# Plain loads and TensorE turns for the first three x, fewer identity products, and shift rows ahead of the second queries

## The reference

```python
qkv = x @ Wqkv + bqkv
q, k, v = jnp.split(qkv, [D, D + KV], axis=-1)          # 16 heads of q, 4 of k and v, tiled to 16
scores = jnp.einsum('bqhd,bkhd->bhqk', q, k) / HD
out = jnp.einsum('bhqk,bkhd->bqhd', softmax(scores), v).reshape(b, s, D) @ Wout + bout
x = layernorm(x + out)
gate, up = jnp.split(jnp.einsum('bsd,hd->bsh', x, ternary_quant(w_gate_up)), 2, axis=-1)
hn = rms_norm(jax.nn.silu(gate) * up)
x = layernorm(x + jnp.einsum('bsh,dh->bsd', hn, ternary_quant(w_proj)))
```

## Time and profile before

| | |
|---|---|
| time, median of 3 runs | 571.05 us (570.61 to 571.38) |
| time of the profiled execution | 570.28 us |
| its span, from the first to the last instruction | 568.3 us |
| mean granted TensorE clock | 0.984 |
| busy in the span | TensorE 92%, VectorE 78%, ScalarE 64%, GpSimd 59% |
| chain that ended last | TensorE 47%, GpSimd 19%, issue 15%, VectorE 10% |

### The profile page before, as it was taken

One profiled execution on the slowest core, in us unless ns is written; L12 is line 12 of the kernel. 1 busy time (PEld: TensorE's weight loads), 2 busy tenths in 40 slices (PEclk: granted clock), 3 DMA queues, 4 the chain that ended last, 5 costly groups with the idle time before them and its releaser, 6 DMA issues.

```text
span 568.3 us, 13548 instructions
## 1 busy us (share of the span) xinstructions
PE 524.5 (92%) x4148; PEld 444.7 (78%) x4148; DVE 442.4 (78%) x1002; ACT 366.0 (64%) x738; POOL 335.5 (59%) x517
## 2 busy tenths in 40 slices
PE   4687999899999999999999999999999999999883
PEld 4677778688888888888888888888888888777772
...
GB/s 227 140 142 123 56 125 76 104 71 110 52 116 60 125 30 145 54 126 73 105 96 100 96 89 107 74 115 63 119 37 155 10 152 48 21 40 1 19 20 37
DMA packets 83379, 49.16 MB, mean 86 GB/s; under 512 B 39680, under 2 KB 83328, under 8 KB 83328
## 3 DMA queue, kind: packets, MB, share of 16 engines
...
## 4 chain that ended last, share of the span: by engine, by line
PE 47%; POOL 19%; issue 15%; DVE 10%; ACT 3%; DMA 3%; SPq 1%; ACTq 1%; POOLq 0%; DVEq 0%
PE ffn_ps L588 12%; PE short_ps L514 8%; PE pv_ps L616 7%; PE short_ps L560 6%; PE exp_ps L569 5%; PE down_ps L601 5%; POOL sq_sum L1015 5%; POOL h_lo L1010 4%; POOL rstd L999 2%; DVE row_max L834 2%; DVE h_f L910 2%; DVE gated L903 2%; POOL attB L403 1%; POOL k_p L1034 1%; DMA q_st<-shift_lo 1%
## 5 line engine op out<-in xcount | busy, mean ns | idle before, releaser
L834 DVE TENSOR_REDUCE row_max<-short_ps 128x2 f32<-128x512 f32 x256 | 174.0, 682 | 60.6 <-PE short_ps L560 60.0
L1010 POOL TENSOR_TENSOR h_lo<-h_f,h_hi 128x256 fp32r<-128x256 f32 x128 | 94.5, 739 | 179.7 <-ACT h_hi L737 179.5
L761 ACT ACTIVATE probs<-exp_ps 128x1024 f32<-128x1024 f32 x128 | 130.7, 1021 | 44.5 <-PE exp_ps L569 43.9
L560 PE MATMUL short_ps<-k_st,q_st 65*128 65x256 f32 x512 | 108.5, 296 | 3.6 <-DVE row_max L834 3.3
L746 ACT ACTIVATE tanh<-ffn_ps 128x256 f32<-128x256 f32 x120 | 45.7, 381 | 96.9 <-PE ffn_ps L588 96.9
L560 PEld LDWEIGHTS short_ps<-k_st,q_st 65*128 65x128 f32 x512 | 88.5, 193 | 15.1 <-issue 2.4
L588 PE MATMUL ffn_ps<-x1T_hi,wguT 128*128 128x256 f32 x480 | 80.8, 291 | 9.9 <-DVE h_f L910 9.3
L569 PE MATMUL exp_ps<-q_st,k_st 67*128 67x512 f32 x256 | 81.6, 400 | 3.3 <-DMA q_st<-shift_lo 3.2
L601 PE MATMUL down_ps<-wpT,h_hi 128*128 128x256 f32 x256 | 79.2, 332 | 3.7 <-POOL h_lo L1010 3.5
L588 PE MATMUL ffn_ps<-x1T_lo,wguT 128*128 128x256 f32 x480 | 78.0, 285 | 0.2 <-DVE x1T_lo L823 0.2
L588 PEld LDWEIGHTS ffn_ps<-x1T_hi,wguT 128*128 128x128 f32 x480 | 65.1, 189 | 16.0 <-issue 10.9
(11 more groups left out here) (104 smaller groups left out, 831.2 us busy)
## 6 DMA issues: line engine op xcount, KB each, us to landing
q_st<-q_dram SPq DMA_DIRECT2D x128, 128.0 KB, 4.1
...
res<-in_L_attn_x_dram SPq DMA_DIRECT2D x16, 256.0 KB, 2.9
out_dram<-y_out SPq DMA_DIRECT2D x16, 256.0 KB, 2.9
...
wgu_raw<-in_L_ffn_w_gate_up_dram SPq DMA_DIRECT2D x8, 256.0 KB, 6.4
...
```

The costliest lines, as they stand in the source:

```text
L560: last = pe.matmul(bank[:, t * S:(t + 1) * S], q_st[0:PAD, st.par, head, t * P:(t + 1) * P], k_st[0:PAD, st.par, st.s % 4, :], start=True, ...
L761: act.activation(probs[:, st.s % 4], exp_ps[:], ACT.Exp).then_inc(exp_done, 1)
L834: dve.tensor_reduce(row_max[:, st.par, head * TT:(head + 1) * TT], short(n, f"max{i}")[:].rearrange("p (t k) -> p t k", t=TT), AX.X, ALU.m ...
L1010: pool.tensor_tensor(h_p[1][:, st.s % 4, :], h_f[:, st.s % 2, :], h_p[0][:, st.s % 4, :].bitcast(F32), ALU.subtract).then_inc(h_lo, 1)
```

## The change

- The first three x (`X_ON_PE` = 3) come by one plain DMA each (`load_plain`, all on SyncE), in whole rows of 1 KB a position. TensorE turns them by four identity products into a short bank (in slots 1, 9 and 17) and ScalarE copies the bank to xT. VectorE's transposes of these three go, and so do ScalarE's two load issues at the start. From the fourth x on all is as it was.
- VectorE's memset of a row of q_st stands at the program's start.
- The DMAs of the shift rows at slot 13 go ahead of the second sequence's first four query loads. The loads of x blocks stand at the end of SyncE's slot, behind keys, queries and shift rows, for every sequence.
- `keep_clock` does nothing in slot 10, and from slot 17 on it puts two products into slots 22 and 24 and none elsewhere.

```diff
 X_T = -1
-FIRST_X_T = 1
+X_T_PE, X_ON_PE = 1, 3
 PROJ_Q = 2
...
-SHORT_ORDER = ("max0", "q", "max1", "sq", "k", "shift0", "o", "shift1", "v", "x1")
-SHORT_OFFSET = {"v": PROJ_V, "q": PROJ_Q, "shift0": SHIFT_T[0], "shift1": SHIFT_T[1],
+SHORT_ORDER = ("max0", "q", "max1", "sq", "k", "shift0", "o", "shift1", "v", "x", "x1")
+SHORT_OFFSET = {"v": PROJ_V, "x": X_T_PE, "q": PROJ_Q, "shift0": SHIFT_T[0], "shift1": SHIFT_T[1],
                 "o": PROJ_O, "k": PROJ_K, "x1": X1_T, "sq": SUM_SQ}
 SHORT_USES = [(m, name) for m in range(SLOTS) for name in SHORT_ORDER
               if name not in SHORT_OFFSET or SHORT_OFFSET[name] % SLOTS == m]
 BANK_TABLE = {0: {"max0": 2, "max1": 1, "sq": 0},
-              1: {"max0": 0, "max1": 2, "shift1": 1},
+              1: {"max0": 0, "max1": 2, "x": 0, "shift1": 1},
               2: {"max0": 2, "max1": 0, "q": 1, "o": 2},
...
 CLOCK_WAIT, CLOCK_LONG = 8, 18
+CLOCK_THIN = 17
 W_POOL_FROM = 4
...
+def x_on_pe(n):
+
+    st = n.once(X_T_PE)
+    return st if st and st.it is None and st.b < X_ON_PE else None
+
+
 def x_turn(n):
-    if n.it is None and n.t == FIRST_X_T:
-        return Step(0, 0, None)
     st = n.once(X_T)
-    return st if st and (st.it is not None or st.b) else None
+    return st if st and (st.it is not None or st.b >= X_ON_PE) else None
...
             st = earlier.once(use[0])
+            if st and use[1] == SHORT_ORDER.index("x"):
+                st = x_on_pe(earlier)
             if st and (back or use[1] < position):
...
             if name == "k" and n.it is None and n.t == PROJ_Q:
-                return short_ps[0]
+                return short_ps[BANK[X_T_PE, "x"]]
             return short_ps[BANK[SHORT_OFFSET.get(name, n.t) % SLOTS, name]]
...
         res_loaded = [sem(f"res_loaded{i}") for i in range(2)]
-        xT_made = sem("xT_made")
+        x_plain = [sem(f"x_plain{i}") for i in range(X_ON_PE)]
+        x_turned, xT_made = sem("x_turned"), sem("xT_made")
         q_made, q_read, q_copied, q_lo = sem("q_made"), sem("q_read"), sem("q_copied"), sem("q_lo")
...
+        def load_plain(eng, b):
+            eng.dma_start(xn[:, b % 2].rearrange("p k n j -> p (k n j)"),
+                          x[b].rearrange("(t p) d -> p t d", p=P)).then_inc(x_plain[b], 16)
+
         def load_blocks(eng, st, group):
...
         def _(sp):
-            for group in range(2):
-                load_blocks(sp, Step(0, 0, None), group)
+            load_plain(sp, 0)
+            load_plain(sp, 1)
             for c in range(W_LATER):
                 sp.dma_start(pieces[c][0], pieces[c][1]).then_inc(w_loaded[c], 16)
-            for group in range(P // BLOCK):
-                load_blocks(sp, Step(1, 0, None), group)
...
                                  ).then_inc(res_loaded[st.par], 16)
-                if st := n.once(STACK_QK):
+                if (st := n.once(STACK_QK)) and not (st.it is None and st.b == 1):
                     sp_wait(q_saved[st.par], st.count2(16, 16))
...
                                  ).then_inc(q_saved[st.par], 16)
-                if (st := n.once(LOAD_X)) and not (st.it is None and st.b < 2):
-                    sp_wait(xT_made, st.count(1, -1))
-                    for group in range(P // BLOCK):
-                        load_blocks(sp, st, group)
                 if st := n.once(STORE):
...
                                 .bitcast(F32), shift_p[half][part][:].bitcast(F32)).then_inc(shift_loaded[half], 16)
+                if n.it is None and n.t == SHIFT_T[0]:
+                    sp.wait_ge(q_saved[1], 16)
+                    stack_queries(Step(1, 0, None), 0)
+                if (st := n.once(LOAD_X)) and not (st.it is None and st.b < 2):
+                    sp_wait(xT_made, st.count(1, -1))
+                    if st.it is None and st.b < X_ON_PE:
+                        load_plain(sp, st.b)
+                    else:
+                        for group in range(P // BLOCK):
+                            load_blocks(sp, st, group)
...
-            released_by = {"v": (v_copied, 1, 1), "q": (q_read, 1, 1), "shift0": (shift_split, 2, 1),
+            released_by = {"v": (v_copied, 1, 1), "x": (xT_made, 1, 1), "q": (q_read, 1, 1), "shift0": (shift_split, 2, 1),
                            "shift1": (shift_split, 2, 2),
...
                 if n.it is not None or not CLOCK_FROM <= n.t < CLOCK_TO:
+                    return
+                if n.t >= CLOCK_THIN and n.t % SLOTS not in (0, SLOTS - 2) or n.t == SLOTS + PROJ_Q:
                     return
...
                     turn_maxima(bank, st, 1)
-                keep_clock(n, 2)
+                if n.t < CLOCK_THIN:
+                    keep_clock(n, 2)
                 if st := n.once(PROJ_V):
...
                     down(st)
+                if st := x_on_pe(n):
+                    bank = use_short(n, "x")
+                    pe.wait_ge(x_plain[st.b], 16)
+                    plain = xn[:, st.par].rearrange("p k n j -> p (k n j)")
+                    turn(bank, [plain[:, t * D + k * P:t * D + (k + 1) * P] for k in range(DT) for t in range(TT)], x_turned)
                 if (c := turned_piece(n, 0)) is not None:
...
         def _(act):
-            for group in range(2, P // BLOCK):
-                load_blocks(act, Step(0, 0, None), group)
             act.dma_start(wqkv[:], Wqkv.rearrange("(t p) n -> p t n", p=P)).then_inc(wqkv_loaded, 16)
...
                     act.activation(probs[:, st.s % 4], exp_ps[:], ACT.Exp).then_inc(exp_done, 1)
+                if st := x_on_pe(n):
+                    wait(act, x_turned, st.count(1, 1))
+                    wait(act, k_made, st.count(1, 0))
+                    high(xT[:], both(n, "x")).then_inc(xT_made, 1)
                 if st := n.once(Q_COPY):
...
             dve.memset(k_st[SROWS:XROWS].bitcast(F32), 1.0).then_inc(k_ones, 1)
+            dve.memset(q_st[SROWS:PAD, 0].bitcast(F32), 0.0).then_inc(q_zeros[0], 1)
...
                 if st := x_turn(n):
-                    wait(dve, x_loaded[st.par], st.count2(64, 64))
+                    wait(dve, x_loaded[st.par], st.count2(64, 64 - 64 * len(range(st.par, X_ON_PE, 2))))
                     wait(dve, k_made, st.count(1, 0))
                     dve.transpose(xT[:].rearrange("p k t -> p (k t)"),
                                   xn[:, st.par].rearrange("p k n j -> p (k n j)")).then_inc(xT_made, 1)
-                    if st.it is None and st.b == 0:
-                        dve.memset(q_st[SROWS:PAD, 0].bitcast(F32), 0.0).then_inc(q_zeros[0], 1)
                 if (c := piece(n, W_MAKE)) is not None:
```

## The result

The changed kernel takes 566.92 us (median of 6 runs, 564.38 to 568.24), beside 570.88 for the kernel before on the same chip. The ratio is 0.9938, with a 95% interval of 0.9917 to 0.996. So it is faster, by 3.5 us and not by the nine that I forecast, and 566.92 lies near the upper end of my range. Five of the six runs lie between 566.8 and 568.24 at mean granted clocks of 0.972 to 0.976; the sixth took 564.38 at 0.985. The profiled execution took 566.8 us, its span 564.9, at a mean granted clock of 0.975.

What follows compares the result with a forecast made beforehand. Bound: waits and slow clock until 56 us, a mixture until 72.5, VectorE until 85.7, TensorE until 99.2. Terms sum to -9.0: 570.28 to 561.3, plus 0.77 is 562.0 us; range 557.5 to 567.5, own range 557.5 to 565.

Steps and rivals of the forecast that it cites:

- Fewer identity products: Slots 17 to 29: removing 48 products gains -1.0 (56.03 to 72.50 us), -0.3 (to 85.72) and -2.4 (to 99.18).
- my other terms: Start -1.5, second and third x +0.3, shift rows ahead of second queries -2.3, clock after that wait -1.8 us.
- Whether the clock holds: VectorE-bound stretch: would TensorE, busy about 60% without the products, keep its clock; the forecast (0.56) took it as holding.
- my first rival: The clock falls once or twice between slots 18 and 25, 1.8 us a fall: 565.6 us, chance 0.22.
- my three terms there (-1.8, -1.0, -0.3): Faster clock after the shift_lo wait, then fewer identity products in 56.03 to 72.50 and 72.50 to 85.72 us.
- The third rival: Clock falls at slot 17, not granted again until feed-forward products at 101 us: 584.8 us, slower than before, chance 0.04.
- The start: Before the first projection: wqkv and x arrive earlier, projection at 6.2 instead of 7.57; -1.5 us (-2.4 to -0.5).
- The second branch: Weights path at the start: w_sum begins behind ScalarE's sign pass at about 8.0, 1.8 us earlier.
- Shift rows and the clock after the wait: Around slot 15's exp scores: TensorE's 2.57 us wait for shift_lo goes (-2.3), the slow stretch behind it shrinks (-1.8).
- They are not late: Second queries and keys, queued behind the shift rows and first read in slot 17, were claimed to arrive in time.
- my second rival: Weights' pieces or VectorE's max reductions pace slots 13 to 16, losing the 2.3 and 1.8: 566.1 us, chance 0.15.
- What I had put at nothing: From the third shift turn (99.18 us before) to the end: same length as before, no gain.

Runs made afterwards that it cites:

- e1: The changed kernel with four identity products again in every slot from 17 on, slot 10 still bare: 565.86 us, ratio 0.9918.
- e11: The changed kernel run again with no edit: 566.25 us, ratio 0.993 to the kernel before.
- e2: The changed kernel with four identity products in slots 17 to 25, none from 26 on, none in slot 10: 564.36 us, ratio 0.989.
- e14: The same kernel as e2, measured again for comparison on one chip: 564.75 us, ratio 0.9884.
- e8: e2 with slot 10's four identity products put back: 565.03 us, ratio 0.9882.
- e13: The changed kernel with two identity products in each of slots 17 to 25 and none from 26 on: 563.81 us, ratio 0.9861.
- e5: The kernel before with only the identity products removed as in the change: 570.67 us, ratio 0.9978.
- e6: The changed kernel with four identity products in slots 17 to 21, a pair each in 22 and 24, none else: 567.82 us, ratio 0.9917.
- e15: The changed kernel without its two pairs, so no identity product from slot 17 on: 568.09 us, ratio 0.994.
- e7: The changed kernel with no identity products in slots 17 to 21, four in 22 to 25, none later: 566.22 us, ratio 0.9912.
- e4: The kernel before with only the x part (plain loads, TensorE turns, ScalarE copies, memset first): 570.06 us, ratio 0.9988.
- e3: The kernel before with only SyncE's new order, shift rows ahead of second queries and x blocks last: 568.12 us, ratio 0.9955.
- e9: e8 with the second sequence's keys issued right behind the shift rows, ahead of its queries: 566.25 us, ratio 0.9934.
- e10: e9 with the old x path, loaded in blocks and transposed by VectorE: 565.61 us, ratio 0.9914.
- e12: e9 with the second x loaded behind the weights and wqkv issued behind the two bias loads: 566.49 us, ratio 0.9937.

## Why the prediction was wrong

The direction was right, and so was the wait that the new order removes. One step failed, the term **"Fewer identity products"** (-1.0, -0.3 and -2.4, together -3.7).

**Fewer identity products.** It was priced as if the clock stayed at 1.00, and that as the likeliest case. What the runs showed: e1, without the thinning, gained 4.7 us of the 5.3 that my other terms add up to, and its interval (3.8 to 5.5) holds the 5.3. With the thinning the gain was 3.5, in e11 4.0. So a term of -3.7 came out at about +1, and that is nearly the whole error of 4.9 us. That the other terms came so near their sum is in part luck: each of them was off by itself, as the next paragraphs say. Where the clock holds, the profiles show less than half of the term's size. From the exp scores of slot 17 to the shift turn before takes 42.8 us and e1 43.1; e2, e14 and e8 take 42.0 to 42.1, e13 41.5. Slots 26 to 29 gave 1.4 to 1.5 us where I had put 2.4, with ends of 1 and 2.9. For slots 17 to 25, where I had put -1.0 and -0.3, they show next to nothing: 29.8 us in e13, 29.7 before. The run times alone allow more: two runs of e5 were 4.3 and 5.1 us under before, and two of e6, which has x and order as well, 7.1 and 7.2, some 2.5 beyond e1; but these are the fastest of twelve and of six, and none of them was profiled.

**Whether the clock holds.** This is my first rival, to which I gave 0.22, and it is what happened. I had the number that should have ruled it up: 60% of TensorE's time busy, where the lowest row at 1.00 had 73%. I let the two pairs outweigh that, and nothing that they do can be seen beside e15. And a row at the full clock was no promise that the clock would stay: in the 13.65 us at 1.00 ahead of the long fall TensorE was busy 9.77, a share like that of the kernel's end. Its price was also too low. I took 1.8 us a fall, from the 6.61 us at 0.56. The long stretch is 13.7 us at the lower level, all of it busy, and from slot 17 to the shift turn the six thinned profiles with a long low stretch (changed, e11, e15, e5, e6, e7; 10.2 to 17.1 us) take 2.6 to 4.6 us more than e13. From the first exp scores to slot 26 the changed kernel gave back 2.3 us on before instead of gaining the 3.1 of my three terms there (-1.8, -1.0, -0.3). The third rival, a clock that never comes back before 101 us, did not occur.

**The start.** -1.5 was too much. The projection came 0.8 us earlier, not 1.4: x landed after 4.2 us beside wqkv and the weights, though it was turned in 1.09 us where I had taken 1.92 for cold. The 1.92 is of a group of four products with eight records; the four turns leave four records, and take 0.60 us in slot 9 (28.69). So the group was the wrong one to price them by. The second branch hardly moved (w_sum -0.3, forecast -1.8). e4's interval for the whole x part is -1.5 to +0.1.

**Shift rows and the clock after the wait.** e3 measured -2.5 [-3.4, -1.7] for what I had put at -2.3 and -1.8. The wait went as said: the exp scores came 2.2 us earlier. The clock gain is there in part. Before, 5.8 us behind the exp scores lie at the lower level. In the profiles with the new order it is 3.4 us in the changed kernel, e2, e7, e9 and e15, and at most 0.1 in the nine others, e3 among them. But this wasn't worth 1.8 us, because another wait took its place: "They are not late", of the second keys, is wrong: e1 waits 1.67 us for them, e3 1.05, e8 1.33, e14 1.20, e13 1.30. They are issued earlier than before, but TensorE is at slot 17 earlier still, and the queries ahead of them take 3.0 to 3.4 us to issue instead of 1.75. From the exp scores of slot 15 to those of slot 17 before takes 6.9 us, e3 5.5, e1 6.2, the changed kernel 6.0; and in slots 17 to 21 e3 takes 17.9 where before took 17.1. That is my second rival in part, at another place.

**What I had put at nothing.** From the third shift turn to the exp scores of slot 31 I had forecast the old length. It fell from 4.80 us to 3.66, and to 4.05 in e1: shift_lo took 3.25 us to land before and ended that stretch, and 1.9 in both of these. That is 0.8 to 1.1 us of the gain which no term holds. e3, with SyncE's order alone, has 5.03 and a landing of 3.5, so the order alone isn't the cause, and I don't know it. The ends of my terms add up to 556.4 and 574.3 us, too, wider than the 557.5 to 565 that I gave as the forecast's own range.

**What stays open.** The lead at the exp scores was 4.5 us in the changed profile, but 3.0 and 2.9 in those of e1 and e2, whose instructions are the same up to there. The 36 records of slot 8 took 4.29 us in the one and 5.77 in e2, where the low clock lay upon them. Where these stretches fall differs from one profile to the next, and I don't know what sets it. Nor do I know why e5's twelve runs split as they did. That e9 is slower than e8 because of the queries is likely by the profiles of e10 and e12, but not shown.
